# A state-space layer with its skip term summed on TensorE and Silu computed by one ScalarE instruction

## The reference

```python
left, right = split(up_x @ W_up + b_up)                  # 128 channels each
x  = silu(conv3(left, conv_w) + conv_b)                  # causal, 3 taps, along the sequence
delta = softplus(x @ W_delta + b_delta)
Bm, Cm = x @ W_B + b_B, x @ W_C + b_C                    # 64 states each
h_t = exp(delta_t * A) * h_{t-1} + delta_t * B_t * x_t   # 128 channels x 64 states
y_t = sum_n h_t[:, n] * C_t[n] + D_skip * x_t
out = (y * silu(right)) @ W_down + b_down
```

## Time and profile before

| | us |
|---|---|
| median of 3 runs | 1945.13 |
| the profiled execution's own time | 1943.71 |
| its span in the trace | 1941.8 |
| state-space layer's own four passes | 1272 to 1744 |

### The profile page before, as it was taken

One profiled execution on the slowest core, in us unless ns is written; L12 is line 12 of the kernel. 1 busy time (PEld: TensorE's weight loads), 2 busy tenths in 40 slices (PEclk: granted clock), 3 DMA queues, 4 the chain that ended last, 5 costly groups with the idle time before them and its releaser, 6 DMA issues. The chain is left out here.

```text
span 1941.8 us, 23851 instructions
## 1 busy us (share of the span) xinstructions
PE 1783.9 (92%) x7605; PEld 939.2 (48%) x7605; DVE 1479.9 (76%) x2434; ACT 900.6 (46%) x2117; POOL 755.0 (39%) x850
## 2 busy tenths in 40 slices
PE   7979999999999899989998999988898988889999
PEld 2346654555555466546665555533332333325555
DVE  5868865555555488757776888689999999998887
ACT  3335544555545455445554333556465554333332
POOL 4832222434333232322220000078989798770000
PEclk9989999999999999979998999989999999899999
DMA  6000000000000000010000000000000000000000
GB/s 254 1 1 1 1 1 1 1 1 1 1 1 1 1 1 1 1 44 1 2 2 1 1 1 1 1 17 6 11 1 17 1 11 6 1 0 1 1 6 17
DMA packets 9787, 20.13 MB, mean 10 GB/s; under 512 B 1088, under 2 KB 8384, under 8 KB 8768
## 3 DMA queue, kind: packets, MB, share of 16 engines
q1 hardware_dynamic: 9664, 18.62, 2.8%
HBM read 14.42 MB, written 1.05 MB: 8 GB/s over the span
## 5 line engine op out<-in xcount | busy, mean ns | idle before, releaser
L2114 POOL TENSOR_TENSOR ssm_hc<-ssm_h,ssm_cm 128x512 f32<-128x512 f32 x256 | 325.4, 1293 | 45.6 <-DVE ssm_h L2171 44.4
L307 PE MATMUL banks<-ffn_x_high,up_high 128*128 128x512 f32 x544 | 282.2, 519 | 10.3 <-ACT ffn_s1g L857 6.2
L2053 PE MATMUL banks<-ssm_hc,const 128*128 128x512 f32 x512 | 272.6, 615 | 5.9 <-DVE ssm_y L2141 5.6
L2171 DVE TENSOR_TENSOR_SCAN ssm_h<-banks,ssm_dbx 128x512 f32<-128x512 f32 x208 | 249.2, 1211 | 10.4 <-issue 7.0
L2098 ACT ACTIVATE banks<-banks,a_neg 128x510 f32<-128x510 f32 x256 | 167.6, 659 | 177.7 <-PE banks L2031 176.5
L308 PE MATMUL banks<-ffn_x_low,up_high 128*128 128x512 f32 x544 | 215.8, 397 | 0.0
L309 PE MATMUL banks<-ffn_x_high,up_low 128*128 128x512 f32 x544 | 215.7, 397 | 0.0
L1504 POOL TENSOR_SCALAR wide_pin<-wide_pin,wide_rden 128x256 f32<-128x256 f32 x256 | 117.6, 478 | 223.1 <-DVE wide_rden L1522 223.1
L343 POOL TENSOR_TENSOR x_norm<-x_centred,x_square 128x512 f32<-128x512 f32 x32 | 41.5, 1298 | 391.8 <-ACT x_square L338 391.8
L1739 ACT ACTIVATE ffn_th<-banks 128x512 f32<-128x512 f32 (+1 forms) x136 | 81.2, 597 | 215.9 <-PE banks L309 193.9
L1160 ACT ACTIVATE rot_pin<-banks,rot_low 128x128 f32<-128x128 f32 (+1 forms) x256 | 104.1, 419 | 100.2 <-DVE rot_low L1242 100.2
(11 more groups left out here) (231 smaller groups left out, 3460.7 us busy)
## 6 DMA issues: line engine op xcount, KB each, us to landing
ssm_packed<-ssm_parts SPq DMA_DIRECT2D x48, 64.0 KB, 2.0
up_whole<-in_up SPq DMA_DIRECT2D x1, 2304.0 KB, 15.3
weights<-in_weights SPq DMA_DIRECT2D x1, 2048.0 KB, 22.6
up_whole<-in_up SPq DMA_DIRECT2D x1, 2048.0 KB, 8.2
half<-in_half SPq DMA_DIRECT2D x1, 1440.0 KB, 18.0
weights<-in_weights SPq DMA_DIRECT2D x1, 1168.0 KB, 25.0
weights<-in_weights SPq DMA_DIRECT2D x1, 1152.0 KB, 8.3
const<-in_const SPq DMA_DIRECT2D x1, 1042.0 KB, 10.3
```

The costliest lines, as they stand in the source:

```text
L307: pe.matmul(out, w_high, x_high, start=True, stop=False)
L2053: pe.matmul(k.bank[5][:], k.c("hot")[:, P - row:2 * P - row], hc[:, i % LAG, :], start=(i % NP == 0), stop=(i % NP == NP - 1)).then_inc(s[ ...
L2114: pool.tensor_tensor(hc[:, i % LAG, :], h[:, i % HOLD, :], cm[:, i // NP % 2, :], ALU.mult) \
L2171: dve.tensor_tensor_scan(h[:, n % HOLD, :], k.bank[DELTA[n % AHEAD]][:], product, 0.0, ALU.mult, ALU.add).then_inc(s["h"], 1)
```

## The change

D_skip becomes a diagonal 128 x 128 matrix. TensorE starts bank 5 of every pass with one f32 matmul of it by xs, and adds the states' sums to that; `finish` is one VectorE multiplication of the bank by the gate; TensorE waits for `gated` where it waited for `y_taken`. ScalarE computes Silu itself, for x straight from the convolution's bank and for the gate from `right`, both in piece 23; the two table loads of passes 1 to 3 stand around them. `natural_log_exp_and_others`, which has Exp too, is active at all other times there. In pass 0, inside the expert layer, the host puts back its own set, and piece 37 needs its load as before. The factor one half and the copies `conv`, `tc`, `y`, `half_b` are gone. x_norm moves from GpSimd's piece 14 to 12; all later pieces of all engines move back by one (17 to 18, ... 56 to 57), and the slot list with them.

```diff
@@ state_space, tensor
-        if n == 17:
+        if n == 18:
             pe.wait_ge(s["n_out"], p + 1)
             pe.matmul(k.bank[7][:], w("left"), k.xn[:, p % 2, :], start=True, stop=True).then_inc(s["left"], 1)
...
-        if n == 21:
+        if n == 22:
             pe.wait_ge(s["right_in"], p + 1)
...
@@ scalar
-        if n == 22:
+        if n == 23:
             act.wait_ge(s["conv"], p + 1)
-            act.wait_ge(s["halved"], 1)
-            act.activation(conv[:], k.bank[7][:], ACT.Identity, bias=half_b[:], scale=0.5).then_inc(s["conv_in"], 1)
-        if n == 21:
-            k.table(act, "exp_and_others")
-        if n == 23:
-            act.wait_ge(s["right_in"], p + 1)
-            act.activation(gate[:, p % 2, :], right[:], ACT.Tanh, scale=0.5).then_inc(s["tanh_r"], 1)
-        if n == 24:
-            act.wait_ge(s["conv_in"], p + 1)
-            act.activation(tc[:], conv[:], ACT.Tanh).then_inc(s["tanh_c"], 1)
+            if p >= 2:
+                act.wait_ge(s["gated"], p - 1)
+            k.table(act, "silu_and_others")
+            act.activation(xs[:, p % 2, :], k.bank[7][:], ACT.Silu, bias=w("conv_b")).then_inc(s["x"], 1)
+            act.activation(gate[:, p % 2, :], right[:], ACT.Silu).then_inc(s["gate"], 1)
+            if p:
+                k.table(act, "natural_log_exp_and_others")
...
@@ gpsimd
-        if n == 14:
+        if n == 12:
             prepare_gpsimd(k, pool, s, p)
...
@@ vector
-        if n == 25:
-            dve.wait_ge(s["tanh_c"], p + 1)
-            dve.scalar_tensor_tensor(xs[:, p % 2, :], tc[:], 1.0, conv[:], ALU.add, ALU.mult).then_inc(s["x"], 1)
-        if n == 27:
-            dve.wait_ge(s["tanh_r"], p + 1)
-            dve.scalar_tensor_tensor(gate[:, p % 2, :], gate[:, p % 2, :], 1.0, right[:], ALU.add, ALU.mult) \
-                .then_inc(s["gate"], 1)
...
@@ reduce
-                if i % NP == 0 and p >= 1:
-                    pe.wait_ge(s["y_taken"], p)
+                if i % NP == 0:
+                    if p >= 1:
+                        pe.wait_ge(s["gated"], p)
+                    pe.matmul(k.bank[5][:], w("skip"), xs[:, p % 2, :], start=True, stop=False)
                 row = 32 * g + c
                 pe.matmul(k.bank[5][:], k.c("hot")[:, P - row:2 * P - row], hc[:, i % LAG, :],
-                          start=(i % NP == 0), stop=(i % NP == NP - 1)).then_inc(s["red"], 1)
+                          start=False, stop=(i % NP == NP - 1)).then_inc(s["red"], 1)
@@ finish
                 dve.wait_ge(s["red"], NP * (p + 1))
-                dve.scalar_tensor_tensor(y[:], xs[:, p % 2, :], w("skip"), k.bank[5][:], ALU.mult, ALU.add) \
-                    .then_inc(s["y_taken"], 1)
-                dve.wait_ge(s["y_taken"], p + 1)
-                dve.scalar_tensor_tensor(gated[:], y[:], 0.5, gate[:, p % 2, :], ALU.mult, ALU.mult) \
-                    .then_inc(s["gated"], 1)
+                dve.wait_ge(s["gate"], p + 1)
+                dve.tensor_tensor(gated[:], gate[:, p % 2, :], k.bank[5][:], ALU.mult).then_inc(s["gated"], 1)
```

More of the change, by code:

```diff
@@ L58, in tables @@
                 ("b_right", 1), ("conv0", P), ("conv1", P), ("conv2", P), ("conv_b", 1), ("b_delta", 1), ("b_b", 1), ("b_c", 1),
-                ("skip", 1), ("b_down", 1), ("a_log", 64)]),
+                ("skip", P), ("b_down", 1), ("a_log", 64)]),
     ]
@@ L1834, in state_space @@
     steps = [i for i in range(ALL) if by_pool(i)]
-    s = k.semaphores("ssm", ["bx", "dx_in", "pdbx", "halved", "cleared", "conv_in", "left", "left_in", "right", "right_in", "tanh_r", "conv", "tanh_c", "x", "delta", "z", "e", "u",
+    s = k.semaphores("ssm", ["bx", "dx_in", "pdbx", "cleared", "left", "left_in", "right", "right_in", "conv", "x", "delta", "z", "e", "u",
                              "ln", "b", "b_in", "c", "c_in", "gate", "ready", "rest", "split", "packed0", "packed1", "packed2", "packed3",
-                             "bc", "a", "da", "dbx", "h", "hc", "red", "y_taken", "gated", "down", "dve", "acts", "resets", "done"] + PREP)
+                             "bc", "a", "da", "dbx", "h", "hc", "red", "gated", "down", "dve", "acts", "resets", "done"] + PREP)
     w = lambda name: k.w(G, name)
@@ L1840, in state_space @@
     home, sb = k.room(number)
-    half_b = sb("ssm_half_b", [P, 1])
     two = lambda ap: ap.rearrange("p (b t) -> p b t", b=NB)
@@ L1844, in state_space @@
     right, gate = sb("ssm_right", [P, T]), sb("ssm_gate", [P, 2, T])
-    conv, tc, xs = sb("ssm_conv", [P, T]), sb("ssm_tc", [P, T]), sb("ssm_xs", [P, 2, T])
+    xs = sb("ssm_xs", [P, 2, T])
     z, e, u, ln, fix = (sb(f"ssm_{name}", [P, T]) for name in ("z", "e", "u", "ln", "fix"))
@@ L1912, in scalar @@
             prepare_scalar(k, act, s, p, 1)
-        if n == 18:
+        if n == 19:
             act.wait_ge(s["left"], p + 1)
@@ L1949, in scalar @@
             act.activation(cm[:, p % 2, :], k.bank[7][:], ACT.Identity, bias=w("b_c")).then_inc(s["c_in"], 1)
-        if n == 37:
+        if n == 38:
             act.wait_ge(s["u"], p + 1)
             act.activation(ln[:], u[:], ACT.Ln).then_inc(s["ln"], 1)
-        if n in (41, 42):
-            v = n - 41
+        if n in (42, 43):
+            v = n - 42
             act.wait_ge(s["ready"], 2 * p + v + 1)
@@ L1959, in scalar @@
             act.activation(parts[:, v, 0, :], (delta, dx)[v][:], ACT.Copy).then_inc(s["split"], 1)
-        if n in (49, 50, 55, 56):
-            part, v = (n - 43) // 6, (n - 43) % 6
+        if n in (50, 51, 56, 57):
+            part, v = (n - 44) // 6, (n - 44) % 6
             act.wait_ge(s["rest"], 4 * p + 2 * (part - 1) + v + 1)
@@ L1965, in gpsimd @@
     def gpsimd(pool, p, n):
-        if n == 14:
+        if n == 12:
             prepare_gpsimd(k, pool, s, p)
-        if n in (45, 46, 51, 52):
-            part, v = (n - 45) // 6, (n - 45) % 6
+        if n in (46, 47, 52, 53):
+            part, v = (n - 46) // 6, (n - 46) % 6
             whole = (delta, dx)[v][:] if part == 0 else rest[:, v, :]
@@ L2004, in run @@
     def run(nxt):
-        y, gated = sb("ssm_y", [P, T]), sb("ssm_gated", [P, T])
+        gated = sb("ssm_gated", [P, T])
         dbx = sb("ssm_dbx", [P, AHEAD, T])
@@ L2009, in run, with programs @@
         with nc.Block(no_gpsimd_drain=True) as block:
-            programs(nxt, block, y, gated, dbx, dxs, pdbx, h, hc)
-    def programs(nxt, block, y, gated, dbx, dxs, pdbx, h, hc):
+            programs(nxt, block, gated, dbx, dxs, pdbx, h, hc)
+    def programs(nxt, block, gated, dbx, dxs, pdbx, h, hc):
         @block.sync
@@ L2351 @@
     lay(5, "b_c", np.concatenate([m["b_C"], m["b_C"]], 0)[:, None])
-    lay(5, "skip", m["D_skip"][:, None])
+    lay(5, "skip", np.diag(m["D_skip"]))
     lay(5, "b_down", m["b_down"][:, None])
```

32 lines of the change are left out of this document (15 added, 17 removed).

## The result

The changed kernel takes **1928.2 us** (median of 4 runs, 1928.12 to 1929.08), beside 1944.82 for the kernel before in 4 runs on the same chip (1942.88 to 1945.4). The ratio on record is 0.9931 with a 95% interval of 0.9905 to 0.9957; it isn't the quotient of the two medians, which is 0.9915. The forecast was 1938.3 us and its range began at 1931.0. The direction was right; the gain of 6.8 us worked out was about half of the measured one, which is 16.6 us by the medians and 13.4 by the ratio. The profiled execution took 1928.22 us (before: 1943.71), with a span of 1926.4.

What follows compares the result with a forecast made beforehand. The prediction took VectorE to bound the layer (busy 112.9 of 118 us in the first pass). Hosted passes gain 7.9 us, edges lose 1.8, the end gains 0.7: 6.8 us faster, so 1938.3 us, range 1931.0 to 1946.0.

Steps and rivals of the forecast that it cites:

- x_norm: Passes 0 to 2: TensorE's wait for x_norm, and VectorE's stall behind it, go; gain 2.86 us a pass.
- The Silu piece: Convolution, passes 0 to 2: load, Silu, Silu, load take 3.8 us; stall 3.9 instead of 2.25, loss 1.7 a pass.
- rival (d): Silu piece: a Silu is two activations' work, 0.6 us more for each of six, 1942.1 us; chance 0.08.
- Rival (b): Silu piece: a load between different activation sets blocks ScalarE for twice its row, 2.56 us; total 1946.0; chance 0.07.
- VectorE's two instructions: Passes 0 to 2: two VectorE instructions of 0.86 and 0.76 us go; gain 1.46 us a pass.
- The end: Behind the last reduce: y leaves the path to the next layer's start; gain 0.7 us.
- The expert layer ahead: Pass 0's pieces: 1.9 us more of ScalarE in one slot; no effect taken, 0.3 us loss as far bound.
- The edge: Between passes, three times: `skip` delays `project` at the lower clock; loss 0.6 us each, bounds 1.27 gain to 1.3 loss.
- rival (a): Edges: TensorE's idle time of 14 us a pass absorbs `skip`; 1.27 us gained three times, 1932.7 us; chance 0.14.
- a change of length outside 1235 to 1750: Sign of being wrong: stages outside 1235 to 1750 on the trace's clock change length.
- Rival (c): x_norm's wait stays because GpSimd or ScalarE comes to it later; 8.6 us not gained, 1946.9 us; chance 0.08.
- rival (e): Behind the Silu piece: TensorE's pause brings the lower clock, five uncovered steps in three passes, 12.8 us, 1951.1; chance 0.06.

Runs made afterwards that it cites:

- run 1: The kernel before with only the skip term moved to TensorE (the fold), Tanh and piece numbers kept: 1936.65 us, ratio 0.9952.
- run 4: The kernel before with only the Silu piece, as piece 22; other pieces at their old numbers, skip term on VectorE: 1941.47 us, ratio 0.9987.
- run 3: The kernel before with only x_norm moved from GpSimd's piece 14 to 12: 1931.79 us, ratio 0.9927.
- run 8: The changed kernel with the skip product issued twice at the three edges, the first result overwritten: 1933.21 us, ratio 0.9938 to the kernel before.
- run 6: The kernel before with x_norm at piece 12 and the skip term on TensorE, Tanh and other pieces kept: 1931.86 us, ratio 0.9926.
- run 7: The changed kernel with the first table load and the gate's Silu moved ahead of the wait for the convolution: 1931.67 us, ratio 0.9921 to the kernel before.
- run 9: The kernel before again, unchanged, one execution for a profile: 1943.84 us.
- run 10: The kernel before with six bf16 products, results unused, in TensorE's pause at the three edges: 1943.77 us, ratio 1.0001.
- run 11: Run 7's kernel with the gated product one instruction earlier on VectorE, ahead of the step's scan: 1927.8 us, ratio 0.9925 to the kernel before.
- run 12: Run 6's kernel with the gated product one instruction earlier on VectorE, ahead of the step's scan: 1928.58 us, ratio 0.993 to the kernel before.
- run 2: The kernel before with x_norm at piece 12 and every piece from 17 on one later, Tanh and y on VectorE kept: 1935.06 us, ratio 0.9944.

## Why the prediction was right and wrong

**x_norm: right.** 2.86 us a pass forecast, 2.87 measured. What I called the stall was two things, 1.1 to 1.4 of waiting and 1.4 to 1.7 of the lower clock behind it (run 1, and passes 1 and 2 of run 4); the sum didn't need them apart, since both go.

**The Silu piece: right as a term of the sum.** Piece 3.8 us forecast, 3.81 measured; loss 1.7 a pass, 1.68 to 1.71 measured. What the prediction didn't see is that moving x_norm alone shortens the stretch of the convolution too, by 0.99 to 1.30 us a pass with Tanh (run 3). Against that kernel the Silu piece, with the shift, costs 2.7 to 3.0 us of stall a pass and saves 1.5 of VectorE's work. The activations of Silu cost what their neighbours cost (0.69 and 0.62 us), so rival (d) falls. Rival (b), a load of twice its row, falls too: the next activation starts 1.29 and 1.30 us after each of the two loads. The Trainium skill's "ScalarE: Activation LUTs", section "What ACT_TABLE_LOAD costs", adds a drain of about 1.38 us to each; the trace disagrees, and the measurement decides. Another statement of that section would have settled rival (d) ahead: every function runs at the same rate, which by its formula makes an estimate of 0.61 us at 512 columns with immediate operands and 0.71 with a pointer to the bias. There the trace agrees (0.62 for the gate, 0.69 for x with its bias).

**VectorE's two instructions: right.** 1.46 forecast, 1.49 to 1.50 measured. **The end: right,** 0.7 and 0.84. **The expert layer ahead: small gain missed.** I took nothing there. TensorE's products outside the layer show 0.4 us gained at about 1240 in all six traces with Silu, and nothing there in the seven traces without it (see below).

**The edge: wrong, and this is the step that failed:** "Loss 0.6 an edge, 1.8 in all". The mechanism was right for an edge with the lower clock. TensorE's queue has no slack left behind `skip` (run 8: 0.87 us for one product more), and where the lower clock follows the pause an edge with the fold costs 0.48 to 0.63, as computed (runs 6 and 7). What was mis-sized is how often it follows, and with it the slack. I read it at the edge of the kernel before, where it came every time (twice three times, run 9), and took it for a property of the pause: 'the delayed `project` now falls into that stretch whole'. With the fold it didn't come at any edge of the changed kernel in two traces, nor of run 1; over all folded edges with the pause of 1.81 us (six of the changed kernel, three each of runs 1, 6, 7 and 8) it came at 4 of 18. Without it the edge gives 1.23: VectorE's whole 1.27 but for 0.04, which was the upper bound and rival (a)'s figure. Rival (a) had the reason in part: `skip` goes into time that TensorE had left, but into that of the edge itself and not into its idle time elsewhere. The 0.7 of slack that the prediction read, by the exponential of the third step and its scan, was what the lower clock had left. At the old edge with the clock up (run 10, first edge: exponential at 1397.63, scan at 1399.93) the same reading gives 1.55; with the fold nothing is left of it, and VectorE waits 0.15. Against a loss of 0.6 each the three edges are 1.83, 1.83 and 1.68 us better: 5.3 of the 6.7 us. So the distance to the forecast is mostly this one term; that the ratio on record still falls inside the range is luck, since its lower end stood there "for a smaller stall at the piece", and that stall came out as computed.

**The last pass: not forecast.** It is 1.38 us shorter, 1.73 of it behind scan 30. The same 1.7 stand in every trace here but those of runs 1, 9, 10 and 11, where the stretches of the lower clock of that pass lie elsewhere. It hangs on where they fall, but what places them isn't shown.

**Outside the layer.** The prediction named a change of length outside 1235 to 1750 as a sign of being wrong. By the starts of TensorE's products outside the layer, the changed kernel was 2.5 us late at 1000 and 1.3 early at 1050, so most of the 1.78 us ahead of the layer arose where nothing was edited. At about 1240, where the expert layer hosts the pieces of pass 0, 0.4 us more were gained; this part belongs to Silu, since it is in all six traces of kernels with Silu and in none of the seven others. The first scan came out between 1.78 us earlier and 2.52 later over the kernels of this study, and 1.26 earlier for the changed kernel again. The other 1.4 us I take for the scatter of single executions; that was not tested further. Rival (c), x_norm's wait staying, and rival (e), the lower clock behind the piece in three passes, didn't happen; rival (e) had its closest case in pass 2, where the stretch at 1538.8 went with 0.40 us more behind scan 30. Its pause behind the piece came in every pass, but over the three traces with this piece in this place (the changed kernel twice, run 8) the lower clock followed it at 2 of 9.

**Part by part.** The move of x_norm gives most, and alone about 4.2 us a pass with what it frees at the convolution (2.87 + 1.30). The fold gives 1.2 an edge where the clock stays up, and 0.84 at the end. The Silu piece is about even against the kernel before (1.5 of VectorE's work for 1.7 of stall, and 0.4 once in the expert layer), but it doesn't pay once x_norm has moved: in scans 21 to 30 the changed kernel is 1.2 to 1.5 us a pass behind runs 3 and 6, which keep Tanh. With half of the piece moved ahead the two are about level (runs 11 and 12). The shift of the other pieces costs with Tanh (runs 2 and 3); whether it pays with Silu wasn't tried.

**Open.** What decides whether the lower clock follows a pause of 1.8 us: at edges with the old pause of 1.87 it came at 6 of 6 in the kernel before, 3 of 3 in run 2, 1 of 3 in run 3 and none in run 4. The runs show only that filling the pause (run 10) or shortening it to 0.70 (runs 11 and 12) left none at nine edges, which is too few to tell from chance where the folded edges as they stood had it at 4 of 18. Whether the 4 us by which the layers of runs 11 and 12 are shorter survive in the whole time would need them timed beside the changed kernel.

## What to carry to other kernels

The lower clock behind a pause of TensorE is no fixed surcharge that a change inherits: write it as a case of its own, with a chance, at every such place before and after the change. Compare traces stretch by stretch on the steps of the bounding engine, where parts agree to 0.05 us while the whole time of one kernel scatters by several, and try each part of a bundled change alone, since here one line gave as much as the bundle. A term that is right against the kernel before can still be a loss beside the other parts of its bundle, as the Silu piece was. In this kernel a long piece of ScalarE did better in ScalarE's wait than behind it: half of the Silu piece moved ahead of its wait made that stretch 1.0 to 1.2 us a pass shorter.

## What the runs showed of the hardware

- A granted clock of 0.50 (1.2 of 2.4 GHz) came behind TensorE's pauses at the same places in two executions of the kernel before; an f32 product over 512 columns in such a stretch took up to 1.91 us (run 7, third edge) where it took 1.02 to 1.10 outside. The same pause of 1.81 us was followed by it at 4 of 18 places.
- A wait of 1.9 us for x_norm cost VectorE 2.86 us with the lower clock behind it and 1.1 to 1.4 without (runs 1 and 4).
- A table load of 1.28 us costs its row and nothing more, from an exponential to Silu as from Silu to an exponential: the next activation starts 1.29 and 1.30 us after the load.
